# A three-layer graph network on one core: lane table in PSUM, 49 node tiles, a shorter carry, and the order check between the statistics chunks

## The reference

```python
def _sage_conv(x, src, dst, Wl, bl, Wr):
    agg = jax.ops.segment_max(x[src], dst, num_segments=x.shape[0])
    agg = jnp.where(jnp.isfinite(agg), agg, 0.0)
    return agg @ Wl + bl + x @ Wr
...
h = jnp.maximum(_layernorm(x, axis=-1), 0.0)
h = leaky_relu(_sage_conv(h, src, dst, Wl1, bl1, Wr1), 0.01)   # 128 -> 256
h = leaky_relu(_sage_conv(h, src, dst, Wl2, bl2, Wr2), 0.01)   # 256 -> 256
h = leaky_relu(_sage_conv(h, src, dst, Wl3, bl3, Wr3), 0.01)   # 256 -> 128
return x + h
```

## Time and profile before

| | |
|---|---|
| median of 3 runs | 6219.27 us (6217.3 to 6219.34) |
| profiled execution | 6222.6 us, its span 6220.9 us |
| POOL busy | 4632.6 us, 74% of the span, 4861 instructions |
| DVE busy | 2902.1 us, 47% |
| PE / ACT busy | 706.5 us / 232.1 us |
| DMA | 1089.93 MB, mean 175 GB/s |

### The profile page before, as it was taken

One profiled execution on the slowest core, in us unless ns is written; L12 is line 12 of the kernel. 1 busy time (PEld: TensorE's weight loads), 2 busy tenths in 40 slices (PEclk: granted clock), 3 DMA queues, 4 the chain that ended last, 5 costly groups with the idle time before them and its releaser, 6 DMA issues. The chain is left out here.

```text
span 6220.9 us, 24572 instructions
## 1 busy us (share of the span) xinstructions
PE 706.5 (11%) x2258; PEld 407.3 (7%) x2258; DVE 2902.1 (47%) x3636; ACT 232.1 (4%) x675; POOL 4632.6 (74%) x4861
## 2 busy tenths in 40 slices
PE   0110011111000680000000000047000000000003
PEld 0000000000000340000000000035000000000002
DVE  5333333333333555555555555565555555555556
ACT  1000000000000110000000000012000000000001
POOL 5777777777777677777777777767777777777776
PEclk8555555555555655555555555565555555555556
DMA  4333333333333576666666666667666666666665
GB/s 131 104 106 106 104 103 105 106 105 104 106 104 103 153 240 210 210 209 212 209 211 209 210 209 209 211 195 252 209 211 209 209 210 209 209 210 211 209 211 166
DMA packets 436613, 1089.93 MB, mean 175 GB/s; under 512 B 101509, under 2 KB 155018, under 8 KB 436586
## 3 DMA queue, kind: packets, MB, share of 16 engines
q0 software_dynamic: 207104, 530.50, 31.0%
q1 hardware_dynamic: 206266, 539.48, 23.2%
q10 hardware_dynamic: 23216, 19.67, 1.0%
HBM read 555.78 MB, written 533.46 MB: 175 GB/s over the span
## 5 line engine op out<-in xcount | busy, mean ns | idle before, releaser
L343 POOL DMA_INDIRECT ring<-features,stage x4692 | 4475.1, 954 | 1491.1 <-issue 1384.2
L638 DVE TENSOR_TENSOR ring<-banks,ring 128x1024 f32<-128x1024 f32 (+1 forms) x1173 | 1226.2, 1045 | 3093.4 <-DMA ring<-features,stage 3076.0
L617 DVE TENSOR_TENSOR banks<-ring,banks 128x1024 f32<-128x1024 f32 (+1 forms) x1173 | 1232.4, 1051 | 37.6
L845 PE MATMUL banks<-ident,ring 128*128 128x128 f32 x20 | 5.0, 428 | 3755.5 <-DVEq L650 3755.5
L827 PE MATMUL banks<-dst_low,own 128*128 128x394 bf16 x200 | 99.2, 496 | 1492.7 <-DVE own L601 1492.7
L845 PEld LDWEIGHTS banks<-ident,ring 128*128 128x128 f32 x20 | 3.9, 222 | 3756.9 <-DVEq L650 3533.0
L811 PE MATMUL banks<-wr,h_turned 128*128 128x256 f32 (+1 forms) x500 | 207.3, 557 | 97.7 <-ACT h_turned L932 97.7
L975 ACT ACTIVATE agg<-zeros 128x512 f32<-128x512 f32 x75 | 47.3, 630 | 3962.2 <-PE banks L876 3962.2
L370 POOL DMA_INDIRECT ring<-running_max_log,end_row x150 | 145.2, 968 | 63.4 <-issue 44.8
L606 DVE COPY stage<-edges 128x8 int32 (+1 forms) x588 | 137.5, 234 | 84.9 <-DVE banks L617 25.8
L813 PE MATMUL banks<-b,ones 1*128 1x256 f32 (+1 forms) x300 | 143.7, 575 | 0.0
(11 more groups left out here) (104 smaller groups left out, 563.7 us busy)
## 6 DMA issues: line engine op xcount, KB each, us to landing
running_max_log<-ring SPq DMA_DIRECT2D x782, 512.0 KB, 3.3
running_max_log<-ring SPq DMA_DIRECT2D x391, 256.0 KB, 2.2
ring<-features,stage POOLq DMA_INDIRECT x4692, 2.8
features<-h_out SPq DMA_DIRECT2D x50, 256.0 KB, 2.3
h_in<-features ACTq DMA_DIRECT2D x100, 128.0 KB
ring<-x SPq DMA_DIRECT2D x5, 640.0 KB, 8.8
features<-ring SPq DMA_DIRECT2D x5, 640.0 KB, 7.2
h_in<-features ACTq DMA_DIRECT2D x50, 64.0 KB
```

What stands on the lines that cost most here:

```text
L343: pool.indirect_dma_start(ring[:, c * w:(c + 1) * w], None, tables[l], bass.IndirectOffsetOnAxis(ap=stage[:, b, u:u + 1].bitcast(U32), axi ...
L617: dve.tensor_tensor(sum_ps[:, 0:CHAINS * w].rearrange("p (h f) -> p h f", h=CHAINS), group(g - 1).rearrange("p (h f) -> p h f", h=CHAINS), ...
L638: dve.tensor_tensor(group(g), sum_ps[:, 0:CHAINS * w], group(g), ALU.max).then_inc(turn, 1)
```

## The change

1. `lane` is also copied to PSUM (`lane_ps`, in the bank of the restart values), and the two comparing picks read it there. The subtracting pick is unchanged.
2. 6250 nodes are 49 tiles (`END_TILES`); the last pair has one tile, in the own term, the end rows, the projections and the output.
3. The join mask and `incoming` are gone: PE turns `carry_scan` itself, shifted by one column; what doesn't join is marked once in the preparation (`alone`). PE starts to turn back as soon as the first half is scanned.
4. `dst`, its neighbours and `src` are loaded from ACT's queue. The order check stands behind the statistics of the first chunk. ACT normalises 7 tiles of a chunk, POOL the other 3, DVE none.
5. In layers 1 and 2 POOL's first step stands outside the loop, and some waits stand in another order.

```diff
-ACT_TILES = 8
+ACT_TILES = 7
+    END_TILES = -(-nodes // P)
+    PAIR_TILES = [min(2, END_TILES - 2 * q) for q in range(PAIRS)]
...
+        lane_ps = banks[:, 5, BANK - 2 * P:BANK]
...
@@ POOL, ahead of the gathers @@
+            for s in range(TAIL_STEPS):
+                share = slice(s * TAIL_TILES + ACT_TILES, (s + 1) * TAIL_TILES)
+                pool.wait_ge(norm_ready, 2 * (s + 1))
+                for k in range(share.start, share.stop):
+                    pool.tensor_scalar(h0_all[:, k, :], x_all[:, k, :], rstd[:, k:k + 1], shift[:, k:k + 1],
+                                       ALU.mult, ALU.add).then_inc(h0_scaled, 1)
+                pool.wait_ge(h0_scaled, (TAIL_TILES - ACT_TILES) * (s + 1))
+                pool.tensor_scalar(h0_all[:, share, :], h0_all[:, share, :], 0.0, None,
+                                   ALU.max).then_inc(h0_rest_done, 1)
...
-                    for b in range(STORES):
+                        for b in reversed(range(STORES)):
                             pool.wait_ge(h_stored[b], PER_OUT * l)
+                        pool.wait_ge(block_scanned, SIGNED * l + 1)
+                        pool.wait_ge(logged[0], LOGGED[0] * l)
...
-                if l == 0:
-                    gather(0, True, False)
-                with pool.Fori(1 if l == 0 else 0, STEPS - 1) as i:
+                gather(0, True, False)
+                with pool.Fori(1, STEPS - 1) as i:
...
-                for b in range(BLOCKS):
+                for b in reversed(range(BLOCKS)):
                     pool.wait_ge(logged[b], LOGGED[b] * (l + 1))
...
-                for t in range(TILES):
+                for t in range(END_TILES):
                     pool.indirect_dma_start(
...
@@ DVE @@
             for s in range(TAIL_STEPS):
                 statistics(s)
-                if s:
+                if s == 0:
+                    check_order()
+                else:
                     normalise(s - 1)
...
-                    dve.tensor_tensor(pick_slot(i), lane[:, :].unsqueeze(1).to_broadcast(across),
+                    dve.tensor_tensor(pick_slot(i), lane_ps.unsqueeze(1).to_broadcast(across),
...
-                    dve.tensor_tensor(not_below[:, :, :], lane[:, :].unsqueeze(1).to_broadcast(across),
+                    dve.tensor_tensor(not_below[:, :, :], lane_ps.unsqueeze(1).to_broadcast(across),
...
-                for c in range(kc):
-                    before = sum(s[0] for s in shapes[:l]) // P
-                    dve.wait_ge(join_step, before + c + 1)
-                    dve.tensor_tensor(incoming[:, c, 1:RUNS], carry_scan[:, c, 0:RUNS - 1],
-                                      join_row[:, 0, 1:RUNS], ALU.add).then_inc(incoming_ready, 1)
...
-                    dve.tensor_tensor(z_sum[b][:, 0:2 * n], mm_ps[b][:, 0:2 * n],
-                                      own[:, q * 2 * n:(q + 1) * 2 * n], ALU.add).then_inc(sum_done, 1)
+                    wide = PAIR_TILES[q] * n
+                    dve.tensor_tensor(z_sum[b][:, 0:wide], mm_ps[b][:, 0:wide],
+                                      own[:, q * 2 * n:q * 2 * n + wide], ALU.add).then_inc(sum_done, 1)
...
+            act.dma_start(dst_runs, dst.rearrange("(h p) j -> p h j", p=P)).then_inc(order_loaded, DMA)
+            act.wait_ge(const_done, 2)
+                for dest, there in run_neighbours(dst):
+                    act.dma_start(dest, there).then_inc(order_loaded, DMA)
+            act.dma_start(src_runs.rearrange("p (h j) -> p h j", h=CHAINS),
+                          src.rearrange("(h p) j -> p h j", p=P)).then_inc(src_loaded, DMA)
```

More of the change, by code:

```diff
@@ L33, with gnn_program @@
 TILE_MASK = 0x7FFFFF80
-def gnn_program(nc, x, src, dst, weights, out):
+def gnn_program(nc, x, src, dst, weights, out, nodes):
     NODES, F_IN = x.shape
@@ L830, in select_run, with select_pair @@
                     mm.then_inc(selected, 1)
-                with pe.Fori(0, PAIRS) as i:
+                def select_pair(i):
+                    pe.wait_ge(pick_ready, i + 2)
+                    for p in range(2):
+                        select_run(i, p)
+                with pe.Fori(0, PAIRS - 1) as i:
                     if l == 0:
-                        pe.wait_ge(pick_ready, i + 2)
-                        for p in range(2):
-                            select_run(i, p)
+                        select_pair(i)
                     own_pair(i)
+                if l == 0:
+                    select_pair(PAIRS - 1)
+                own_turn(PAIRS - 1, 0)
+                own_project(PAIRS - 1, 0)
                 if l == 0:
@@ L859, in turn_pair @@
                         pe.wait_ge(agg_done, PAIRS * l + q - 2)
-                    for t in range(2):
+                    for t in range(PAIR_TILES[q]):
                         k = 2 * q + t
@@ L956, in count_run, with keep_pair @@
                                          accum_out=below[:, bass.ds(j * 2 + p, 1)]).then_inc(below_counted, 1)
-                def keep_pair(j, more):
+                def keep_pair(j, loads):
                     if l == 0:
@@ L961, in keep_pair @@
                             count_run(j, p)
-                    for p in range(2):
-                        keep_turned(j, p, more)
+                    for p in range(PAIR_TILES[j] if isinstance(j, int) else 2):
+                        keep_turned(j, p, p < loads)
                         keep_own(j, p)
@@ L984, in _ @@
                 sp.dma_start(x_all[:, t, :], x_rows[:, t, :]).then_inc(x_loaded[s], DMA)
-                if s == 0:
-                    sp.dma_start(dst_runs, dst.rearrange("(h p) j -> p h j", p=P)).then_inc(edges_loaded, DMA)
-            sp.dma_start(src_runs.rearrange("p (h j) -> p h j", h=CHAINS),
-                         src.rearrange("(h p) j -> p h j", p=P)).then_inc(edges_loaded, DMA)
-            sp.wait_ge(const_done, 2)
-            with nc.allow_non_contiguous_dma(reason="one word of each run of edges"):
-                for dest, there in run_neighbours(dst):
-                    sp.dma_start(dest, there).then_inc(edges_loaded, DMA)
             for l, (wl, bl, wr) in enumerate(weights):
@@ L1071 @@
     }
-    out = nc.dram_tensor("out", (rows, arrays["L0_gnn_Wl3"].shape[1]), F32, kind="ExternalOutput").ap()
+    out = nc.dram_tensor("out", (-(-nodes // P) * P, arrays["L0_gnn_Wl3"].shape[1]), F32, kind="ExternalOutput").ap()
     weights = [tuple(given[name] for name in layers[3 * l:3 * l + 3]) for l in range(3)]
-    gnn_program(nc, given["x"], given["src"], given["dst"], weights, out)
+    gnn_program(nc, given["x"], given["src"], given["dst"], weights, out, nodes)
     r = run_bass_kernel_spmd(nc, [arrays], core_ids=[0])
```

174 lines of the change are left out of this document (90 added, 84 removed).

## The result

| | before | after |
|---|---|---|
| median of 4 runs each, us | 6218.74 (6217.3 to 6219.34) | 6178.9 (6178.24 to 6179.73) |
| profiled execution, us | 6222.6 | 6178.24 |
| its span, us | 6220.9 | 6176.4 |

A forecast was written before the change was run, and what follows sets the result against it. POOL's row of indirect DMAs was taken as the bound, with DVE waiting. Terms 33.5 + 8.3 + 3.2 = 45.0 us off the profiled 6222.6 gave 6177.6, a median of 6174.3, range 6163 to 6187.

The forecast's parts named there:

- Picks from PSUM: First layer's 25 pick steps: two comparing picks with a PSUM operand no longer stretch POOL's gathers, saving 33.5 us.
- 49 tiles: Layer ends: one gather fewer per layer (3.75 us in all) and shorter tails behind the last gather, together 8.3 us.
- the queue ahead that I had laid end to end: Layer ends: the full pair's four DVE operations queue between the last pair's; first layer's tail 3.7 us, 1.6 less.
- Shorter carry: Carry between layers: hidden by the patch rows' transfer with 2.5 us to spare, so removing the join gains 0.
- Opening and order of waits: Layer openings and POOL's reordered waits: instructions cost at most some tenths of a us; gain 0, 1 us either way.
- The start: Before the first gather: earlier stores move it from 40.13 to 36.6 us, a gain of 3.5, taken as 3.2.
- swallow the wait of 1.56 us: Start, DVE's statistics: the moved order check fills the 1.56 us wait ahead of the second chunk; statistics change by +0.4 us.
- The 1.4: Start: POOL's time from the last feature store's landing to the first gather, put at 1.4 us.
- The late loads: Rival at the start: the order check waits for its small loads; start loses about 6 us, median 6183; chance 0.13.
- POOL's tiles: Start: POOL's three tiles take 1.3 us a chunk, hidden under DVE's 3.1; as a rival bound, 6238 us, chance 0.02.
- a sign of being wrong: Start: POOL's element instructions of more than 0.8 us would show the prediction wrong.

The follow-up runs named there:

- picks_sbuf: The changed kernel with the two comparing picks reading the lane table from SBUF again, as before the change: 6219.21 us, 35.6 more than after_again.
- tiles50: The changed kernel with 50 node tiles in each layer again, so every pair has two: 6194.13 us, ratio 0.9946 to the kernel before.
- after_again: The changed kernel unedited, run once more beside the first group of experiments: 6183.6 us, ratio 0.9932 to the kernel before.
- after_third: The changed kernel unedited, run once more beside the third group of experiments: 6191.59 us, ratio 0.9933 to the kernel before.
- carry_padded: The changed kernel with a DVE row addition put back after each half of the carry's scan, which PE waits for: 6185.62 us, ratio 0.9933 to the kernel before.
- waits_plain: The changed kernel with POOL's waits in the old code order and the semaphore increment ahead of the end rows put back: 6188.61 us, 5.0 more than after_again.
- check_last: The changed kernel with the order check behind the statistics of all chunks, as before the change: 6174.44 us, 9.2 less than after_again.
- picks_all: The changed kernel with the upper pick table also in PSUM, so the subtracting pick has one SBUF operand: 6180.5 us, ratio 0.9924 to the kernel before.
- words_first: The changed kernel with the order check's neighbour words issued ahead of dst on ACT's queue: 6190.38 us, against 6191.59 for after_third.

## Why the prediction was right, and where its terms were not

**The sum.** Between the two profiled executions the time fell by 44.4 us, forecast 45.0. The median is 4.6 us above the forecast 6174.3, and that is the step from the execution to the median: I carried over that the profiled run lies 3.3 us above it, and after the change it lay 0.7 us below. That the sum itself is within 0.6 us is luck in part, as the terms show.

**Picks from PSUM, 33.5 us: right.** 35.25 us by the trace, 35.6 us by `picks_sbuf`. The gathers of the first layer say where it comes from. In the kernel before 49 of them take 1.53 to 1.75 us, 33.8 us above 944 ns in all, and after the change none does: that is the term as summed. The ones beside the subtraction lose 3.2 us in place of 4.1, and the stretched ones at the start of the layer 0.6 less than before, which makes up the rest. The mean gather is 946 ns where picks run, as I asked for. L619's gather starts 0.32 us behind it and not 0.42, and in the step shown it takes 1.18 us against 1.08.

**49 tiles, 8.3 us: right in size, by partly wrong steps.** From the last end-row gather to the last h_out it was 8.84, 10.24 and 8.59 us, and is 6.69, 8.62 and 7.68 us: 2.15 + 1.62 + 0.91 = 4.7 us, forecast 4.55 as 1.6 + 1.85 + 1.1. With the 4.45 us of the end rows themselves (3.75 for three gathers, and 0.7 in the spacing of the others) that is 9.1, and `tiles50` says 8.8. The 0.7 is not a gain of the tiles: the end rows take 182.7 us in `after`, but 184.1 in `after_again` and 183.6 in `after_third`. The end of the second layer:

```profile
4130.22 0.69 DVE L754 TENSOR_TENSOR z_sum<-banks,own 128x512 f32<-128x512 f32 x1 [0.23 <-PE banks L901]
4130.94 0.69 DVE L766 SCALAR_TENSOR_TENSOR h_out<-z_sum 128x512 f32<-128x512 f32 x1
...
4132.00 0.42 DVE L766 SCALAR_TENSOR_TENSOR h_out<-z_sum 128x256 f32<-128x256 f32 x1
```

Here DVE works off the full pair ahead, two operations of 0.69 us, and then the half-wide ones of 0.42: the queue ahead that I had laid end to end. In the third layer that queue hid more of the gain than I had put.

**Shorter carry, 0: right,** by `carry_padded`.

**Opening and order of waits, 0 with 1 us either way: wrong, it gained 5.** The step that failed is that the instructions between a release and a gather make up "at most some tenths of a us". The waits ahead of the patch and the increment ahead of the end rows cost about 0.6 us at each of six gates (the first layer's patch apart), and the row for it was in the trace of before: 0.72 us of issue behind two waits in its chain. I had read the gap as POOL's reaction, and had not counted that the increment went. `waits_plain` shows all of it at 5.0 us, 4.3 of them at the six gates. In the first layer the gap ahead of the patch did not shrink (6.33 and 6.29 us): DVE's last maximum started 2.55 us behind the last gather's start before (2033.17 to 2035.72) and 3.15 behind it after (2003.82 to 2006.97), since the gather landed later, and from there to the patch gather it is 3.78 and 3.14. Why it landed later I didn't try.

**The start, -3.2 us: wrong, it lost 5.9.** The step that failed is "swallow the wait of 1.56 us": I let the check move in DVE's queue and fill the gap ahead of the second chunk, as if its loads were there. They were not, which I had only as a rival. Step by step against the forecast first gather of 36.6: the wait for the loads 8.0 us; `x` later by 2.1 us (5.55 to 7.63) instead of 1, 1.1; POOL's last part ends 2.2 behind ACT's; 0.4 of these 11.3 us is made good in between, so that the last store comes 10.9 us late (42.0 in place of 31.1); the landing at 3.7 and not 4.1, and POOL's reaction at 0.3 and not 1.4, give 1.5 back. 36.6 + 10.9 - 1.5 = 46.0. The 1.4 was a misreading: the last store before landed 7.7 us behind its issue, not the median 7.2, and POOL's reaction was 0.9. The stores themselves went as forecast, each as its chunk was ready, and landed in 3.6 to 3.8 us.

**The rivals.** The late loads had 0.13 and 6183. Their mechanism is what happened at the start, with the first gather 5.9 us late, where I had said about 6. The time came out lower because the other terms gave more than summed. So my forecast hit with errors that nearly cancel: the start is 9.1 us short (+5.9 for -3.2), and over it are the picks by 1.8 (35.25 for 33.5), the tiles by 0.8 (9.1 for 8.3) and the waits by about 6, which is what is left of 44.5 - 45.0 + 9.1 - 1.8 - 0.8 and holds the 4.0 us of the gaps around the patch and what lies behind the last h_out.

**POOL's tiles: hidden but for the last chunk, and dearer than my rows.** A chunk takes about 2.5 us, where I had 1.3 by rows, and the 384-element operation with its 1.16 to 1.18 us is above the 0.8 that I had named as a sign of being wrong. The profile's groups have 578 ns for the 128-element operation and 1271 ns for the 384-element one, with the last, stretched chunk in them:

```profile
L273 POOL TENSOR_SCALAR ring<-ring,rstd,shift 128x128 f32<-128x128 f32 x15 | 8.5, 578 | 25.3 <-DVE shift L444 25.3
L276 POOL TENSOR_SCALAR ring<-ring 128x384 f32<-128x384 f32 x5 | 6.4, 1271 | 0.4
```

By the rate that the Trainium skill, GPSIMD Engine Reference (Elementwise — side-by-side cycle accounting), gives for two-input work, a chunk is 1.7 us as an estimate; the trace is above that too, though these operations read one tile each. The page keeps element work on VectorE, and the trace agrees that it is faster there: 0.60 us for two tiles and 0.29 for 256 elements. Up to the last chunk it is hidden: 2.5 lies under the 3.1 us that DVE needs. At the end it isn't: POOL is done 2.2 us behind ACT, and in `check_last` 1.3 us behind it (32.70 and 31.41).

## What to carry to other kernels

Before a check or a copy is moved earlier in an engine's queue, ask when its input lands while everything else loads: the wait is paid by all that is queued behind it, and here changing the order of its loads didn't help. Where one engine issues indirect DMAs for the whole span, look at what the others do while one of them starts: one operand from PSUM instead of SBUF took 35 us off a kernel whose VectorE was busy for 47% of it. At a gate of several semaphores look in the chain for what is recorded between the last landing and the DMA, and don't trust the order in the code: here the wait that passes last had to stand first there, with no increment behind it. Other orders were not run.

## What the runs showed of the hardware

- An indirect DMA on POOL is held by a DVE operation that reads both operands from SBUF: 0.94 us becomes 1.53 to 1.75 beside the f32 comparisons of 1.22 us, and 1.18 in the step shown beside the bf16 subtraction of 0.68 us. With one operand in PSUM it is not held at all, in the same phase (0.94 to 0.95). The Trainium skill, SBUF — State Buffer (Who interferes with whom), states this: a DVE instruction with two SBUF inputs contends with a GpSimd instruction that reads SBUF, and one with at most one SBUF input does not, outside DVE's 2-port perf modes. By that rule `picks_sbuf` and `picks_all` come out as they did, and the trace agrees.
- One SBUF operand alone is no safeguard: the gather of 4.53 us runs on through L555, a TENSOR_SCALAR with one SBUF operand, and ends 0.11 us behind it. What that operation costs alone no run shows.
- Two waits recorded between the last release and an indirect DMA (the first can be the released one itself) move it from 0.26 to 0.88 us behind the release, one semaphore increment moves it to 0.82. Their own 0.04 us each in the chain don't tell this.
- POOL's element operations are stretched beside DVE's single-operand copies too: 3.28 us for three operations that took 1.30, beside `L529 COPY`. In `check_last`, where the last chunk is done before that copy starts (at 33.08), the same three take 1.31, and those beside the check's comparison L452, which reads two SBUF operands, take 2.91.
- One of the eight small loads of neighbouring words took 4.74 us to issue on ACT's queue, as one took 4.54 on SP's; the other seven took 0.33 to 0.72 on the same queue. In `words_first`, with nothing ahead of them, the longest took 2.09, and `dst` behind them 4.35. What makes one issue long and not the next no run shows.
